# Scan of the first decoder layer: the products that sum over the states are spread over seven of a unit's eight slots, and the copies of the sums stand two slots later

## The reference

```python
def step(h, inputs):
    d_t, B_t, C_t, u_t = inputs
    dA = jnp.exp(d_t[:, :, None] * A)
    h = h * dA + (d_t * u_t)[:, :, None] * B_t[:, None, :]
    y_t = jnp.einsum('bdn,bn->bd', h, C_t)
    return (h, y_t)
...
y = jnp.transpose(ys, (1, 0, 2)) + u * D
```

## Time and profile before

| | us |
|---|---|
| median of 3 runs | 1419.47 (1418.7 to 1422.88) |
| profiled execution, own time | 1428.01 |
| its span in the trace | 1426.0 |
| mean granted TensorE clock, share of full speed | 0.813 |
| first scan of a tile starts | 80.7 |
| last scan of a tile starts | 413.9 |
| busy time of PE, DVE, POOL, ACT over the span | 1109.9, 849.1, 569.8, 529.4 |

### The profile page before, as it was taken

One profiled execution on the slowest core, in us unless ns is written; L12 is line 12 of the kernel. 1 busy time (PEld: TensorE's weight loads), 2 busy tenths in 40 slices (PEclk: granted clock), 3 DMA queues, 4 the chain that ended last, 5 costly groups with the idle time before them and its releaser, 6 DMA issues. The chain is left out here.

```text
span 1426.0 us, 29397 instructions
## 1 busy us (share of the span) xinstructions
PE 1109.9 (78%) x11843; PEld 810.9 (57%) x11843; DVE 849.1 (60%) x1500; ACT 529.4 (37%) x1322; POOL 569.8 (40%) x382
## 2 busy tenths in 40 slices
PE   3478999989987989897455598599376999856795
PEld 1167888888873544555345255445365454543595
DVE  7576888888855674466512476557413486755233
ACT  2433444444332553353123163156133575612121
POOL 5079898999836503110345210010434101001332
PEclk9656888787787798999579698789578798977898
DMA  2098788777755000000273100000364000000783
GB/s 103 14 231 204 202 208 210 207 202 199 202 187 172 2 1 0 1 1 1 62 207 107 30 1 1 1 1 2 130 199 158 1 1 1 2 1 22 248 291 104
DMA packets 74229, 139.72 MB, mean 98 GB/s; under 512 B 8128, under 2 KB 28368, under 8 KB 73744
## 3 DMA queue, kind: packets, MB, share of 16 engines
q1 hardware_dynamic: 70128, 129.67, 32.2%
q0 software_dynamic: 3968, 8.18, 1.6%
HBM read 128.06 MB, written 14.82 MB: 100 GB/s over the span
## 5 line engine op out<-in xcount | busy, mean ns | idle before, releaser
L648 ACT ACTIVATE shifted_a<-scores,nmax_a 128x128 f32<-128x128 f32 x768 | 208.6, 387 | 90.9 <-DVE nmax_a L614 90.9
L1115 PE MATMUL decay<-delta,A_pairs 32*128 32x127 f32 x2048 | 183.5, 344 | 43.5 <-DVE small_pack L1209 15.9
L1190 ACT ACTIVATE decay<-decay 128x1016 f32<-128x1016 f32 x128 | 128.8, 1010 | 201.0 <-PE decay L1115 201.0
L1115 PEld LDWEIGHTS decay<-delta,A_pairs 32*128 32x128 f32 x2048 | 160.7, 243 | 64.1 <-DVE small_pack L1209 20.4
L614 DVE TENSOR_REDUCE nmax_a<-scores 128x4 f32<-128x512 f32 x192 | 123.7, 686 | 114.2 <-PE scores L553 111.9
L355 POOL TENSOR_TENSOR rstd<-ve,neghalf 128x4 f32<-128x4 f32 x30 | 31.5, 1050 | 283.9 <-DVE ve L341 283.9
L620 DVE COPY PTs_a<-PT 128x512 f32<-128x512 f32 x192 | 123.7, 682 | 3.2 <-PE PT L561 3.1
L1450 POOL DMA_INDIRECT results<-xs_s x76 | 72.9, 959 | 119.2 <-DVE xs_s L1619 108.8
L561 PE MATMUL PT<-mamba_pack,shifted_a 128*128 128x128 f32 x768 | 114.8, 295 | 3.5 <-DVE PTs_a L620 2.7
L561 PEld LDWEIGHTS PT<-mamba_pack,shifted_a 128*128 128x128 f32 x768 | 89.2, 150 | 37.5 <-issue 21.9
L1101 POOL TENSOR_TENSOR pos_bias<-pos_bias,B 128x1024 f32<-128x1024 f32 x36 | 85.2, 2383 | 10.0 <-DMA pos_bias<-du_rows 10.0
(11 more groups left out here) (391 smaller groups left out, 2192.7 us busy)
## 6 DMA issues: line engine op xcount, KB each, us to landing
pos_bias<-du_rows SPq DMA_DIRECT2D x72, 256.0 KB, 4.8
small_pack<-L3f_w SPq DMA_DIRECT2D x15, 768.0 KB
XN<-du_rows SPq DMA_DIRECT2D x38, 256.0 KB, 4.8
XNT<-du_rows SPq DMA_DIRECT2D x38, 256.0 KB, 4.8
O<-du_rows SPq DMA_DIRECT2D x36, 256.0 KB, 4.9
masked_cos<-du_rows SPq DMA_DIRECT2D x36, 256.0 KB, 4.8
masked_sin<-du_rows SPq DMA_DIRECT2D x36, 256.0 KB, 4.8
small_pack<-L2f_w SPq DMA_DIRECT2D x15, 514.0 KB
```

The source lines that it names most:

```text
L648: t = nc.scalar.activation(shifted[u % 4][:, j, :], scores[u % 4][:, j, :], ACT.Exp, scale=-1.0, bias=nmax[:, u % 4, j:j + 1])
L1115: t = nc.tensor.matmul(decay[k % DEEP][:, s, i, 1:S], A_pairs[strip, c, 4 * q + i, :, :].rearrange("p j n -> p (j n)"), delta[strip, c, b ...
L1190: nc.scalar.activation(x, x, ACT.Exp).then_inc(decayed, 1)
```

## The change

A unit's products are cut into 7 parts (`PARTS`) of 4 or 5 turns in place of 4 parts of 8 turns, and stand in slots 8n + 11 to 8n + 17. `turn_back` moves from slot 8n + 17 to 8n + 19, and within a slot it now stands ahead of the products. On ACT `copy_sum`, `copy_y` and `place_c` stand two slots later. The first part of unit n now waits for the copied sum of unit n - 1, where it waited for that of unit n - 2. The number of instructions is the same.

```diff
-    UNITS, PER, DEEP = B * IC, 8, 3
+    UNITS, PER, DEEP, PARTS = B * IC, 8, 3, 7
...
-                    if n >= 2:
-                        pe.wait_ge(sum_copied, n - 1)
-                half = part // 2
-                for turn in range(8 * (part % 2), 8 * (part % 2) + 8):
+                    if n >= 1:
+                        pe.wait_ge(sum_copied, n)
+                for turn in range(32 * part // PARTS, 32 * (part + 1) // PARTS):
+                    half = turn // 16
...
-                if part == 3:
+                if part == PARTS - 1:
                     t.then_inc(summed, 1)
...
-            for k in range(TILES + 18):
+            for k in range(TILES + 20):
                 if k < TILES:
                     multiply(k)
-                if k >= 11 and (k - 11) % 8 < 4 and (k - 11) // 8 < UNITS:
-                    gather((k - 11) // 8, (k - 11) % 8)
-                if k >= 17 and (k - 17) % 8 == 0 and (k - 17) // 8 < UNITS:
-                    turn_back((k - 17) // 8)
+                if k >= 19 and (k - 19) % 8 == 0 and (k - 19) // 8 < UNITS:
+                    turn_back((k - 19) // 8)
+                n, part = (k - 11) // 8, (k - 11) % 8
+                if 0 <= n < UNITS and part < PARTS:
+                    gather(n, part)
...
-                if k % 16 == 8 and 0 < k // 16 < B:
+                if k % 16 == 10 and 0 < k // 16 < B:
                     place_c(k // 16)
-                if k >= 15 and (k - 15) % 8 == 0 and (k - 15) // 8 < UNITS:
-                    copy_sum((k - 15) // 8)
-                if k >= 18 and (k - 18) % 8 == 0 and (k - 18) // 8 < UNITS:
-                    copy_y((k - 18) // 8)
+                if k >= 17 and (k - 17) % 8 == 0 and (k - 17) // 8 < UNITS:
+                    copy_sum((k - 17) // 8)
+                if k >= 20 and (k - 20) % 8 == 0 and (k - 20) // 8 < UNITS:
+                    copy_y((k - 20) // 8)
```

More of the change, by code:

```diff
@@ L1125, in gather @@
                     pe.wait_ge(c_placed, b + 1)
-                    if n >= 2:
-                        pe.wait_ge(sum_copied, n - 1)
-                half = part // 2
-                for turn in range(8 * (part % 2), 8 * (part % 2) + 8):
+                    if n >= 1:
+                        pe.wait_ge(sum_copied, n)
+                for turn in range(32 * part // PARTS, 32 * (part + 1) // PARTS):
+                    half = turn // 16
                     for i in range(4):
-                        token = 64 * half + 16 * i + turn
+                        token = 64 * half + 16 * i + turn % 16
                         t = nc.tensor.matmul(Y[32 * i:32 * i + 32, n % 2, half, :], Cz[:, token, :],
-                                             at_token[n % 2][:, :, token], start=(turn == 0), stop=(turn == 15))
-                if part == 3:
+                                             at_token[n % 2][:, :, token], start=(turn % 16 == 0), stop=(turn % 16 == 15))
+                if part == PARTS - 1:
                     t.then_inc(summed, 1)
@@ L1185, in _ @@
             place_c(0)
-            for k in range(TILES + 19):
+            for k in range(TILES + 21):
                 if k < TILES:
```

## The result

The changed kernel took 1447.19 us (median of 4 runs, 1444.14 to 1457.2), the one before 1421.18 (4 runs, 1418.7 to 1427.8): a ratio of 1.018, 95% interval 1.0149 to 1.0211. It is 26 us slower, where 34.5 were forecast.

The account below looks back on a forecast made before the run. PE's late multiplies were taken to bound the scans: 23.4 us a unit against 21.15 gives + 33 us over 14.6 units, + 34.5 with the end, so 1419.5 becomes 1454 us. Range 1432 to 1478, for 8 in 10 1424 to 1486.

Parts of the forecast that it names:

- x: Share of scan time with TensorE's granted clock at 1.00: 0.58 before, 0.3 chosen for the change, bounds 0.1 to 0.5.
- the prediction's own formula: Time of a unit (8 tiles) with PE bounding throughout: 1 / (x / 18.9 + (1 - x) / 26.0) us.
- (a): Three more switches between multiplies and products on PE: 0.32 us each at 1.00, 0.28 at 0.50.
- (b): Scan of tile 8n waits for the later last products, idling PE 1.45 us a unit at 1.00, about 0.5 at 0.50.
- (c): Copies on ACT, two slots later: the first part's new wait for the previous unit's copied sum costs nothing.
- (d): End of the scans: last products 1.5 us later; reload of `small_pack` may slip POOL's first read 2 to 3 us, taken as 0.
- Falls once a unit: TensorE's clock falls about once a unit as before, at PE's 1.45 us idle between two bare multiplies.
- Rises: TensorE's clock rises later or not at all in a unit, since the new slots hold products only 37% at 0.50.
- It never rises: Rival: TensorE's clock stays at 0.50, 26.0 us a unit, + 71 us and 2 at the end: 1492; chance 0.15.
- It stays at 1.00: Rival: TensorE's clock holds at 1.00 throughout, 18.9 us a unit, 33 us less: 1388; chance 0.10.
- 8 tiles, a unit, cost at least 18.5 us: Floor of the scan stretch, from POOL feeding a tile every 2.31 us; units cost 21.15 us before the change.

Follow-up runs that it names:

- e5: The changed kernel unaltered, run again on another chip: 1451.92 us, 1.0158 of the kernel before.
- e4: The changed kernel with products reading other data (A_pairs) and the scan of tile 8n not waiting for them: 1387.63 us, 0.9854 of the kernel before.
- e6: The changed kernel with products reading other data (A_pairs), the scan of tile 8n still waiting for them: 1453.78 us, 1.0186 of the kernel before.
- e9: The changed kernel with the same parts one slot earlier (8n + 10 to 8n + 16), turning back and copies too: 1399.79 us, 0.9853 of the kernel before.
- e1: The changed kernel with products in four parts of 8 turns again, its other moves kept: 1420.56 us, 1.0077 of the kernel before.
- e2: The changed kernel with the turning back one slot earlier, in the slot without products: 1475.76 us, 1.0453 of the kernel before.
- e7: The changed kernel with parts of 8 and six times 4 turns, products, turning back and copies one slot earlier: 1398.14 us, 0.9797 of the kernel before.

## Why the prediction was right

**Direction and mechanism held, the size in the main; the share of time at 1.00 was set too low.** The step that was mis-sized is "For x I choose 0.3". It was 0.5 in the first trace (clock 0.75 from 106 to 415 us) and about 0.38 in e5 (0.69). With x = 0.5 the prediction's own formula gives 21.9 us a unit, measured 22.10; with 0.38 it gives 22.8, measured 22.92. With x = 0.5 the prediction has 12.5 us more than before, with 0.38 it gives 22.8 - 21.15 = 1.65 for each of 14.6 units and 1.5 at the end, 25.6 more. Measured were 16.2 between the two spans at x = 0.5, and 26 and 23 between the medians of the two chips. That the forecast of 34.5 looks close beside 26 owes something to chance: between the two profiled executions it is twice the 16.2. The scan of tile 127 starts at 426.65 us in the first trace, where 447 was named, and the mean clock is 0.75 and 0.69 where 0.65 was.

- **The rows' prices held.** (a) A slot with 5 turns takes 2.32 us at 1.00 (192.22 to 194.54; forecast 2.3) and 3.26 at 0.50 (143.26 to 146.52; 3.25).
- (b) PE's idle time behind the held scan is 1.42 us at 1.00 and 0.50 at 0.50, forecast 1.45 and 0.5. A unit at 0.50 takes 26.2 us, forecast 26.0. The shortest take 20.0 to 20.1, forecast 18.9 for one at 1.00: none is at 1.00 throughout, each holds a fall of about two slots, which the difference of 1.2 us fits.
- What (b) left out is that the stall has a second price, the clock. The prediction named the stall as the place of the fall, but priced it with the 1.45 alone and put the rest into x. e4 against e6 and e9 against the change show the sum: 3%.
- (c) The copies cost nothing: from 106 to 415 us PE waits for none of them. The turning back, moved with them, seems not to be free where PE has room elsewhere (e1, 0.8%); the prediction priced its work but not its place.
- (d) The last products start 1.3 us later; 1.5 were forecast. The pause of 3.03 us among them was not. POOL's first read stands 3.0 us further behind the last scan than before, as much as was allowed for the reload, but it is the products and the pause that did it.
- **Falls once a unit** came as forecast: at 1.00 the clock fell behind the stall in each unit (197 to 202 us, PE busy 72%). **Rises** were more frequent than x = 0.3 has them: the first came at 183 us, far later than before (106 us), but from then on the turning back with the first part beside it brought the clock up in all but two units (in e5 in all but five, from 156 us on). e2 shows that this neighbourhood is what kept the change from the 1492 of "It never rises". e2, which takes it away, is that rival: 66 us over before, where 71 and 2 were worked out for it.
- The rival "It stays at 1.00" fell with the changed kernel, but e7 is its scan nearly as drawn: 17.5 to 18.4 us in ten units, 31 us less than before where 33 were worked out.
- "8 tiles, a unit, cost at least 18.5 us" holds only on the average. Single units of e7 take 17.5, which POOL's pace of 2.31 a tile allows only if it had got ahead in the slower units before. Over e7's fourteen units it is 19.2, and in e4 the units settle at 18.6 to 18.7, so little is left to gain on PE alone.

What stays open: why the clock comes up in one unit and not in the next with the same instructions (units of 20.1 and of 24.9 us stand side by side); single runs of the change differ by 1%; and the pauses of PE without a releaser.

## What to carry to other kernels

When work is spread over more slots, ask first who waits for its last piece: here a buffer's reuse, two units on, cost more than the spreading could give, and the same spreading one slot earlier gained 1.5% (e9). A stall on TensorE can be paid twice, as here: in itself and in the clock behind it; price it with what a unit costs at the other level too, not by its length alone. Where an engine's clock depends on what it does, the order of equal work is a cost of its own, and it needs a run to find it.

## What the runs showed of the hardware

- TensorE busy 100% for 294 us at a granted clock of 0.50 (e2), with 16 matmul records of 32 rows and 32 to 40 of 128 rows in turn; the same records in another order had a mean of 0.75 (the change) and 0.90 (e7, with parts of 8 and 4).
- The products (128 x 32 weights, 64 columns) take the same time at both levels, 1.30 and 1.32 us for 40 records, while the multiplies double, 1.16 and 2.07 us for 16.
- TensorE paused 1.2 to 3.0 us now and then, within one run of matmuls and with no releaser (3.03 us at 437.86 in the changed kernel, 1.24 at 422.11 before).
